# Shifted-window attention and a spiking layer: maxima and their addition as 64 by 64 products in one stretch

## The reference

```python
attn = jnp.einsum('wihd,wjhd->whij', q, k)
attn = attn + bias[None, None] + MASK[None, :, None]
out = jnp.einsum('whij,wjhd->wihd', jax.nn.softmax(attn, axis=-1), v)
x = x + attention(group_norm(x)); x = x + lif(group_norm(x) @ W.T + b)
```

## Time and profile before

| | |
|---|---|
| median of 3 runs | 546.38 us (544.23 to 547.46) |
| the profiled execution: its time | 547.18 us |
| its span (first to last instruction) | 545.5 us |
| busy in the span: TensorE / its weight loads | 467.2 / 424.0 us |
| busy: VectorE / ScalarE / GpSimd | 426.9 / 395.2 / 272.0 us |
| TensorE's granted clock, mean over the span | 0.969 |

### The profile page before, as it was taken

One profiled execution on the slowest core, in us unless ns is written; L12 is line 12 of the kernel. 1 busy time (PEld: TensorE's weight loads), 2 busy tenths in 40 slices (PEclk: granted clock), 3 DMA queues, 4 the chain that ended last, 5 costly groups with the idle time before them and its releaser, 6 DMA issues.

```text
span 545.5 us, 17534 instructions
## 1 busy us (share of the span) xinstructions
PE 467.2 (86%) x6504; PEld 424.0 (78%) x6504; DVE 426.9 (78%) x864; ACT 395.2 (72%) x885; POOL 272.0 (50%) x369
## 2 busy tenths in 40 slices
PE   0274699988999899989999998999899977889996
PEld 0274588878889788979888997988789876778885
DVE  6846567876888788878887898788778767578897
ACT  2275578876888788878887897888789845755551
POOL 6133475557555755666556666655756536520000
PEclk9988789998999999999999999999999979889999
DMA  6267067775676677767876776666566645023333
GB/s 191 79 164 183 12 168 184 180 179 156 184 180 176 171 180 210 192 161 198 197 191 164 192 200 177 173 166 161 154 161 176 175 108 145 3 77 136 135 135 136
DMA packets 92574, 86.07 MB, mean 158 GB/s; under 512 B 41842, under 2 KB 63604, under 8 KB 92532
## 3 DMA queue, kind: packets, MB, share of 16 engines
q1 hardware_dynamic: 91808, 85.49, 58.7%
q10 hardware_dynamic: 724, 0.01, 0.1%
HBM read 47.72 MB, written 33.55 MB: 149 GB/s over the span
## 4 chain that ended last, share of the span: by engine, by line
PE 37%; POOL 13%; issue 13%; DMA 12%; ACT 10%; DVE 6%; SPq 6%; ACTq 1%; POOLq 1%; DVEq 0%
POOL p_lo L426 6%; DMA k_stack<-k_spill1lo 5%; PE pv_ps L1005 4%; SPq L311 3%; POOL xn_lo L388 3%; PE score_ps L892 3%; DMA k_spill1lo<-k_lo 3%; PE score_ps L982 3%; PE proj_ps L892 3%; PE pv_ps L892 3%; PE proj_ps L905 2%; POOL xc L415 2%; PE proj_ps L907 2%; PE proj_ps L906 2%; PE score_ps L972 2%
## 5 line engine op out<-in xcount | busy, mean ns | idle before, releaser
L426 POOL TENSOR_TENSOR p_lo<-probs,p_hi 128x512 f16<-128x512 f32 x128 | 146.6, 1167 | 154.8 <-ACT p_hi L580 154.8
L972 PE MATMUL score_ps<-both_parts,bias_k 128*128 128x64 f16 x1024 | 82.8, 194 | 11.5 <-DMA k_stack<-k_spill1lo 7.3
L579 ACT ACTIVATE probs<-score_ps 128x512 f32<-128x512 f32 x128 | 76.9, 600 | 19.7 <-PE score_ps L982 18.9
L905 PE MATMUL proj_ps<-xn_hi,w_hi 128*128 128x256 f32 x256 | 77.1, 301 | 14.2 <-POOL xn_lo L388 14.2
L972 PEld LDWEIGHTS score_ps<-both_parts,bias_k 128*128 128x128 f16 x1024 | 67.4, 98 | 20.9 <-issue 8.4
L974 PE MATMUL score_ps<-q_stack,k_stack 96*128 96x64 f16 x1024 | 82.0, 193 | 0.0
L756 DVE TENSOR_REDUCE neg_max<-max_ps 128x16 f16<-128x1024 f32 x64 | 78.4, 1225 | 4.2 <-PE max_ps L955 2.2
L580 ACT ACTIVATE p_hi<-score_ps 128x512 f16<-128x512 f32 x128 | 77.3, 604 | 0.0
L906 PE MATMUL proj_ps<-xn_lo,w_hi 128*128 128x256 f32 x256 | 73.8, 288 | 0.0
L907 PE MATMUL proj_ps<-xn_hi,w_lo 128*128 128x256 f32 x256 | 73.8, 288 | 0.0
L974 PEld LDWEIGHTS score_ps<-q_stack,k_stack 96*128 96x128 f16 x1024 | 69.5, 98 | 0.0
(11 more groups left out here) (136 smaller groups left out, 1352.7 us busy)
## 6 DMA issues: line engine op xcount, KB each, us to landing
xc<-in_x_dram SPq DMA_DIRECT2D x32, 256.0 KB, 4.8
k_stack<-k_spill0hi SPq DMA_DIRECT2D x32, 256.0 KB, 4.2
k_stack<-k_spill1hi SPq DMA_DIRECT2D x32, 256.0 KB, 4.0
out_dram<-xc SPq DMA_DIRECT2D x32, 256.0 KB, 2.3
q_hi<-q_flat SPq DMA_DIRECT2D x128, 32.0 KB, 2.0
k_spill0hi<-k_hi SPq DMA_DIRECT2D x16, 256.0 KB, 2.2
k_spill0lo<-k_lo SPq DMA_DIRECT2D x16, 256.0 KB, 2.4
q_stack<-q_spill0hi SPq DMA_DIRECT2D x32, 128.0 KB, 2.8
```

What stands on the lines that cost most here:

```text
L426: pool.tensor_tensor(p_lo[p][:, quads, :, :].rearrange("p g w i -> p (g w i)"), probs[:, quads, :, :].rearrange("p g w i -> p (g w i)"), p ...
L579: act.activation(probs[:, quads, :, :].rearrange("p g w i -> p (g w i)"), score_ps[:, h, :], ACT.Exp)
L905: pe.matmul(dst, w_hi[:, c, cols], high[:, tok], start=(c == 0 and bias is None), stop=False)
L972: pe.matmul(dst, bias_k[:, variant(k, w), h * QUADS + g, :], both_parts[:, 0, :], start=(g == 0 and w == 0), stop=False)
```

## The change

- `max_scores`: each product of 128 by 128 becomes four of 64 by 64 (rows: the quads 0, 1 or 2, 3 of a half, "mid"; columns of the array: the queries of one quad, "q"). The two mids write different banks, and the columns that are one window's in a bank are 256 wide. Eight products of 256 columns bring in the bias, sixteen of 128 columns the scores.
- The addition of the maxima: likewise, sixteen products of 64 by 64 with 128 columns in place of eight. Both banks of `score_ps` are signalled by the last products.
- The banks of `score_ps`, and with them p_hi and p_lo, go by mid in place of half.
- `neg_max` has 128 columns (8 of maxima and 56 zeros for each mid); its transpose is 128 by 128 and the copy to `max_rows` takes all 128 partitions.
- Order on TensorE: `max_scores` of the next pair stands directly behind the addition of the maxima, ahead of `weigh_values`. All waits of the two are taken ahead of the last score product. On VectorE `maxima` of the next pair stands ahead of `attention_out`.
- Setup: other layouts of `bias_q` and `pick_max`, and one more memset.

```diff
-        pick_max = sb("pick_max", [128, 2 * QUADS, 128], f16)
+        pick_max = sb("pick_max", [128, 2 * HALVES, 128], f16)
-        bias_q = sb("bias_q", [128, 4, QUADS, 128], f16)
+        bias_q = sb("bias_q", [128, 4, 2, HALVES, 128], f16)
-        neg_max = sb("neg_max", [128, 16], f16)
+        neg_max = sb("neg_max", [128, 128], f16)
...
-            for buf in max_rows:
+            for buf in (max_rows[0], max_rows[1], neg_max):
...
-                act.activation(max_rows[p][0:16, :], max_ps[:, 0, :].bitcast(f16)[0:16, 0:128], ACT.Copy)\
+                act.activation(max_rows[p][:, :], max_ps[:, 0, :].bitcast(f16)[:, 0:128], ACT.Copy)\
...
-                dve.tensor_reduce(neg_max[:, :], max_ps[:, :, :].rearrange("p w (n j) -> p (w n) j", j=WS), AX.X, ALU.max,
+                dve.tensor_reduce(neg_max[:, :].rearrange("p (m n) -> p m n", m=2)[:, :, 0:8],
+                                  max_ps[:, :, :].rearrange("p m (n j) -> p m n j", j=WS), AX.X, ALU.max,
...
+                if not is_last_pair(n):
+                    maxima(n + 1)
                 beside = None
...
                 if not is_first(n, 1):
                     attention_out(n - 1, (k - 1) % 4, beside)
-                if not is_last_pair(n):
-                    maxima(n + 1)
...
-            def max_scores(m, row, k):
-
-                slot = k // 2 % 2
+            def await_max_operands(m, row, k):
+
                 if k % 2 == 0:
                     pe.wait_ge(k_hi_done, row + 1)
-                    pe.wait_ge(q_spread[slot], slot_total(row, k // 2, 64))
-                wait(pe, max_rows_done, m)
+                    pe.wait_ge(q_spread[k // 2 % 2], slot_total(row, k // 2, 64))
                 if is_first(m, 8):
                     pe.wait_ge(bias_q_done, variant(k, 1) + 1)
+
+            def max_scores(k):
+
+                slot = k // 2 % 2
+                halves = [slice(r * WS, (r + 1) * WS) for r in range(2)]
                 for w in range(2):
-                    pe.matmul(max_ps[:, w, :], ident_h[:, :], bias_q[:, variant(k, w), :, :].rearrange("p m n -> p (m n)"),
-                              start=True, stop=False)
+                    for mid, rows in enumerate(halves):
+                        for q, queries in enumerate(halves):
+                            pe.matmul(max_ps[queries, mid, w * 256:(w + 1) * 256], ident_h[rows, rows],
+                                      bias_q[rows, variant(k, w), q, :, :].rearrange("p h n -> p (h n)"),
+                                      start=(w == 0), stop=False)
+                for w in range(2):
                     wx = 2 * (k % 2) + w
                     for h in range(HALVES):
-                        for mid in range(2):
-                            at = (2 * h + mid) * 128
-                            last = pe.matmul(max_ps[:, w, at:at + 128],
-                                             q_hi[slot][:, h, wx, 2 * mid:2 * mid + 2, :].rearrange("p q i -> p (q i)"),
-                                             k_hi[slot][:, h, wx, :, :].rearrange("p e j -> p (e j)"),
-                                             start=False, stop=(h == 1 and mid == 1))
+                        at = (2 * w + h) * 128
+                        for mid, rows in enumerate(halves):
+                            for q, queries in enumerate(halves):
+                                last = pe.matmul(max_ps[queries, mid, at:at + 128], q_hi[slot][rows, h, wx, 2 * mid + q, :],
+                                                 k_hi[slot][rows, h, wx, :, :].rearrange("p e j -> p (e j)"),
+                                                 start=False, stop=(w == 1 and h == 1))
...
-            def scores(n, row, k):
+            def scores(n, row, k, before_tiles):
...
+                                if (mid, h, q, w) == (1, 1, 1, 1):
+                                    before_tiles()
...
-                pe.wait_ge(max_rows_done, n + 1)
-                for h in range(HALVES):
-                    for w in range(2):
-                        for mid in range(2):
-                            dst = score_ps[:, h, :].rearrange("p (m q w i) -> p m w q i", m=2, q=2, w=2)[:, mid, w, :, :]
-                            last = pe.matmul(dst, pick_max[:, 4 * w + 2 * h + mid, :],
-                                             max_rows[p][:, :].rearrange("p (q i) -> p q i", q=2),
-                                             start=False, stop=(w == 1 and mid == 1))
-                    last.then_inc(score_ps_done, 1)
+                halves = [slice(r * WS, (r + 1) * WS) for r in range(2)]
+                for w in range(2):
+                    for h in range(HALVES):
+                        for mid, rows in enumerate(halves):
+                            for e, keys in enumerate(halves):
+                                dst = score_ps[keys, mid, :].rearrange("p (h q w i) -> p h w q i", h=2, q=2, w=2)[:, h, w, :, :]
+                                last = pe.matmul(dst, pick_max[rows, 2 * w + h, keys],
+                                                 max_rows[p][rows, :].rearrange("p (q i) -> p q i", q=2),
+                                                 start=False, stop=(w == 1 and h == 1))
+                            if w == 1 and h == 1:
+                                last.then_inc(score_ps_done, 1)
...
+                def await_tile_operands():
+                    pe.wait_ge(max_rows_done, n + 1)
+                    if not is_last_pair(n):
+                        await_max_operands(*following)
+
+                scores(n, row, k, await_tile_operands)
...
+                if not is_last_pair(n):
+                    max_scores(following[2])
                 if not is_first(n, 1):
                     weigh_values(n - 1, row if p else row - 1, (k - 1) % 4, beside)
-                if not is_last_pair(n):
-                    max_scores(n + 1, row + 1 if p else row, (k + 1) % BODY)
```

More of the change, by code:

```diff
@@ L634, in _ @@
             dve.wait_ge(mask_step, 6)
-            dve.tensor_copy(pick_max[:, :, :].rearrange("p v (e j) -> p (v e) j", e=2),
-                            ident_h[:, 0:16].unsqueeze(2).to_broadcast([128, 16, WS]))
+            for r in range(2):
+                half = slice(r * WS, (r + 1) * WS)
+                dve.tensor_copy(pick_max[half, :, :].rearrange("p v (e j) -> p (v e) j", e=2),
+                                ident_h[half, r * WS:r * WS + 8].unsqueeze(2).to_broadcast([WS, 8, WS]))
             for buf in (v_hi[1], v_lo[1]):
@@ L965, in scores @@
                     pe.wait_ge(stacked[slot], slot_total(row, k // 2, 96))
-                for h in range(HALVES):
-                    wait(pe, p_hi_done, n * 2 + (h - 1))
-                    for g in range(QUADS):
-                        for w in range(2):
-                            dst = score_ps[:, h, g * 128 + w * WS:g * 128 + (w + 1) * WS]
-                            at = h * WCOLS + 2 * p + w
-                            pe.matmul(dst, bias_k[:, variant(k, w), h * QUADS + g, :], both_parts[:, 0, :],
-                                      start=(g == 0 and w == 0), stop=False)
-                            pe.matmul(dst, k_stack[slot][:, g, at, :], q_stack[slot][:, g, at, :], start=False, stop=False)
-                    if h == 0:
-                        turn_maxima(n)
@@ L977, in scores @@
-                pe.wait_ge(max_rows_done, n + 1)
-                for h in range(HALVES):
-                    for w in range(2):
-                        for mid in range(2):
-                            dst = score_ps[:, h, :].rearrange("p (m q w i) -> p m w q i", m=2, q=2, w=2)[:, mid, w, :, :]
-                            last = pe.matmul(dst, pick_max[:, 4 * w + 2 * h + mid, :],
-                                             max_rows[p][:, :].rearrange("p (q i) -> p q i", q=2),
-                                             start=False, stop=(w == 1 and mid == 1))
-                    last.then_inc(score_ps_done, 1)
+                for mid in range(2):
+                    wait(pe, p_hi_done, n * 2 + (mid - 1))
+                    for h in range(HALVES):
+                        for q in range(2):
+                            for w in range(2):
+                                col = (2 * h + q) * 128 + w * WS
+                                dst = score_ps[:, mid, col:col + WS]
+                                at = h * WCOLS + 2 * p + w
+                                pe.matmul(dst, bias_k[:, variant(k, w), h * QUADS + 2 * mid + q, :], both_parts[:, 0, :],
+                                          start=(h == 0 and q == 0 and w == 0), stop=False)
+                                if (mid, h, q, w) == (1, 1, 1, 1):
+                                    before_tiles()
+                                pe.matmul(dst, k_stack[slot][:, 2 * mid + q, at, :], q_stack[slot][:, 2 * mid + q, at, :],
+                                          start=False, stop=False)
+                    if mid == 0:
+                        turn_maxima(n)
```

13 lines of the change are left out of this document (7 added, 6 removed).

## The result

| | before | after |
|---|---|---|
| median | 546.38 us | 582.70 us (579.63 to 588.88) |
| ratio | | 1.0684, 95% interval 1.0645 to 1.0724 |
| busy: TensorE / VectorE / ScalarE / GpSimd | 467.2 / 426.9 / 395.2 / 272.0 us | 460.7 / 423.0 / 392.7 / 272.6 us |
| granted clock, mean | 0.969 | 0.916 |

No engine has noticeably more to do than before, and the kernel is 36 us slower. Ratios are formed from the undisturbed executions of both kernels; the profiled one of the kernel after, 588.88 us, is the longest of its five and not among them (its clock is 0.916, that of the others 0.923 to 0.935). Lines in what follows are those of the kernel after: L984 and L988 are the scores, L998 the addition of the maxima, L957 and L966 the maximum scores, L1006 the transpose of the maxima, L1022 the values, L1032 the attention's turn, L908 to L910 the projections.

What follows compares the result with a forecast made beforehand. TensorE was taken to lead, with the other engines close behind. Four rows (one sample) shrink from 51.51 to 50.42 us, 1.09 less; over 8 samples 8.7 us, giving 538 us, range 529 to 552.

Steps and rivals of the forecast that it cites:

- The change part by part: Step pricing tiles, layout borders, waits, signals and VectorE's order; saved 0.18 us per pair, 0.19 more at the transpose.
- Rival D: Tile stretch: 64-column loads without the fast way, or tiles waiting for one another, 40 ns per tile; 561 us, chance 0.18.
- The tile's price: 40 products of 64 by 64 per pair: 24 ns each, 0.96 us, the middle between 16 and 32 ns.
- case B: Tile stretch: all four quarters of the array work at once, 16 ns per tile; 532 us, chance 0.22.
- the borders of the stretch: Changing the array's layout going in and out of the tiles: 0.20 us added, bounds 0 and 0.4.
- The transpose: Transpose of the maxima, made 128 wide, no longer changes the array's layout: 0.19 us saved, bounds 0 and 0.19.
- Waits taken earlier: Tiles wait for the next pair's q_hi and k_hi about 1.2 us sooner: nothing, up to 1 us if q_hi slips.
- 0.55 for p = 0: TensorE's wait for ScalarE's copy of the maxima at p = 0, lengthened from 0.36 to 0.55 us.
- The row of the roots: Row with the norm's roots (k = 2 and 3), hanging on ScalarE's exponentials and GpSimd: 14.35 to 14.55 us.
- VectorE's order: Maxima ahead of attention_out remove a 0.65 us wait, but projections still wait for GpSimd's xn_lo: counted 0.

Runs made afterwards that it cites:

- order_only: Kernel after with its order, waits, banks and 128-wide transpose, but products of the maxima and their addition 128 by 128 as before; 579.19 us, ratio 1.0621.
- tiles_hint: Kernel after plus a hint for TensorE at the loop's head that its last branch will be taken; 550.31 us, ratio 1.0039.
- before_slot239: Kernel before, work unchanged, head of TensorE's loop placed 239 instructions into a block of 256; 585.54 us, ratio 1.0744.
- tiles_unrolled: Kernel after with TensorE's loop over the five middle samples written out, so without a jump back; 559.31 us, ratio 1.0212.
- before_unrolled: Kernel before with TensorE's loop written out, so without a jump back; 552.46 us, ratio 1.01.
- order_hint: Kernel after with its new order but wide products instead of tiles, and the jump back announced to TensorE; 548.78 us, ratio 1.0051.
- picks_head0: Kernel after with only the additions as tiles, maximum scores wide, and the loop's head on the border of a 256-instruction block; 554.33 us, ratio 1.0198.

## Why the prediction was wrong

I gave 538.0 us, range 529 to 552, and 0.17 for slower. It is 582.7.

**The step that failed** is "The change part by part": it counts what 40 products cost on the array and nothing for their instructions, so the path from one pass to the next has no term in the sum. A load and a matmul for each of 40 products in place of 18, for the eight pairs of a pass, are 22 x 2 x 8 = 352 instructions, which is the whole growth from 1610 to 1962. The 32 more of order_only were enough by themselves: what decides is whether the loop runs on into an eighth block, with its jump not announced. No case had this. No row of before showed a price for it, but the page had the resource: the instruction queue, which brought nothing between 160 and 360 us before, and 31 blocks after. Rival D, slower, got its direction by luck and was wrong in its mechanism: neither the loads nor tiles waiting for one another cost anything that the rows show. The loss: 3.2 us of waiting at each of four ways back, the clock at 0.50 behind it (the row from 227.39 takes 14.30 at 0.79, in tiles_hint the row at that place 12.23), and keys that land late in the same pass (4.2 us of waits, 1.2 in tiles_hint's four rows; why the keys are later I did not trace). Together 61.5 against 51.4 us per pass.

**The tile's price** was case B's: 16 additions in 0.25 us, 24 maximum scores in 0.55, where I took 24 ns each. I had counted 0.20 for the borders of the stretch, and that was right: from the last score product to the first addition it is 0.13, where products of one layout follow in 0.03, and from the last tile to the first value 0.15, where the next group of tiles follows in 0.05. The Trainium skill, "TensorEngine Tiling (Array Packing)", section "Tile-to-Partition Mapping" (no fast weight load in an array split by columns), would have made it case D; the trace doesn't show that cost. The Trainium skill, "TensorE: Matmul & The Clock Gate", section "Part 3: Packing small matmuls — row/col tiling", is nearer with its 4 ns or so from tile to tile: the four of a group start 3 to 4 ns apart. From one group to the next it is 56 ns (80 behind the first of the additions), and that sets the 0.25 us for 16.

**The transpose**: 0.28 became 0.09 (221.20 to 221.29), the 0.19 I took. Right.

**Waits taken earlier**: q_hi's transfers nowhere show. But ScalarE's copy of the maxima now is late for both pairs of a row: 1.5 us in five waits in a pass. In the row from 290.03 of tiles_hint, which nothing else disturbs, the last score product starts 0.67 us after the one before it at p = 0 and 0.33 at p = 1, where 0.03 is usual: 0.64 and 0.30 lost. I had 0.55 for p = 0 and nothing for p = 1. With the tiles' 0.05 more per pair that is the difference between this row's 11.45 us and the 10.97 of my steps for case B.

**Case B's rows against tiles_hint**, which is the change without its code's cost: 10.97, 11.66, 11.96, 15.08 predicted, 12.91, 11.75, 12.23, 14.50 measured. Rows 2 and 3 are right to 0.3. The row of the roots was taken 0.6 too long: I added 0.53 to it for the keys, and it shows no wait for them. Row 1 is 1.9 too short, 1.46 of it with the clock's fall. The step is "VectorE's order": I saw that the 0.65 at the transpose would turn up at the projections and counted 0. True for that row; I did not ask what one long idleness does that two short ones don't.

**What the rest gives**: 51.39 for 51.51, so the change without its code makes no difference, 1.0039 (0.9986 to 1.0091).

## What to carry to other kernels

Count the instructions of an engine's loop before unrolling or splitting products in it, and look at the instruction queue in the profile: a wait on "issue" at the first instruction of a pass, with new transfers on that queue, was code here and not work. Announcing the jump back took it away, and so did keeping the loop within seven blocks by placing its head; where 352 more instructions leave no such place, only the first is left. When an engine gets quicker but its wait for another gets longer, look at the granted clock behind the wait. And try the same cure on the kernel before: the best part here, GpSimd's order, had nothing to do with the change.

## What the runs showed that was not expected

- A loop of unchanged work costs 546 or 585.5 us by where its head lies (before, before_slot239). 57 instructions into the eighth block all four ways back wait, 26 into it only some.
- Straight code fetched from memory hardly stops TensorE: 62 transfers and one "issue" wait of 2.5 us in tiles_unrolled, ahead of the loop's place, against four of about 3.2 in the loop. The 1% of before_unrolled is not in such waits.
- The announced loop of 1962 instructions goes round with no transfer between 160 and 360 us, the same loop unannounced has 31.
- The idle stretches of 2.5 us at the projections are followed by the 1.2 GHz level in four of five cases in tiles_hint, those of 1.55 to 1.57 in none of order_hint's six. The length alone does not decide: behind 1.72 us in picks_head0 the clock fell once in six times (at 244.27; the mean over the next 6 us is 0.72), and behind 1.69 in tiles_unrolled (187.12) it did too.
- Products of 64 by 64 in the four quarters of the array run side by side: 40 of them in 0.80 us, with loads of 64 columns at no visible cost.
